# A small vision tower on one core: layer 0's attention outputs and sums computed by token, divided there and turned

## The reference

```python
def _L0_attn_ref(hidden_states, Wq, Wk, Wv, Wo):      # 16 heads of 16
    q = proj(Wq) * d ** (-0.5)
    k = proj(Wk)
    v = proj(Wv)
    s = jnp.einsum('bhqd,bhkd->bhqk', q, k)
    attn = 1.0 + s + 0.5 * s * s
    attn = jnp.where(causal, attn, 0.0)
    o = jnp.einsum('bhqk,bhkd->bhqd', attn, v)
    z = jnp.sum(attn, axis=-1, keepdims=True) + EPS   # 1e-6
    o = o / z
    y = o.transpose(0, 2, 1, 3).reshape(b, t, dim)
    return y @ Wo.T
```

## Time and profile before

| | us |
|---|---|
| median of 3 runs | 287.32 (284.48 to 288.15) |
| the profiled execution | 285.78 |
| its span | 284.1 |
| mean granted clock of PE, share of full | 0.988 |

### The profile page before, as it was taken

One profiled execution on the slowest core, in us unless ns is written; L12 is line 12 of the kernel. 1 busy time (PEld: TensorE's weight loads), 2 busy tenths in 40 slices (PEclk: granted clock), 3 DMA queues, 4 the chain that ended last, 5 costly groups with the idle time before them and its releaser, 6 DMA issues.

```text
span 284.1 us, 8057 instructions
## 1 busy us (share of the span) xinstructions
PE 250.1 (88%) x3292; PEld 197.7 (70%) x3292; DVE 182.9 (64%) x347; ACT 152.0 (54%) x322; POOL 157.2 (55%) x227
## 2 busy tenths in 40 slices
PE   0779989957999899897997899999999997988983
PEld 0667878845888688686886788888888884434331
DVE  0534628511559999999998588988777785534111
ACT  1312102056898868776765166675657653833450
POOL 7441324544374988787889556868676661145000
PEclk9999999999999999999999689999999999999999
DMA  5899430000000000000000000000000000002021
GB/s 176 202 248 310 106 98 0 3 0 0 3 2 2 0 2 2 2 2 3 3 2 0 2 2 2 3 3 2 3 2 5 2 3 2 0 0 68 0 66 44
DMA packets 9897, 9.81 MB, mean 35 GB/s; under 512 B 4303, under 2 KB 9030, under 8 KB 9862
## 3 DMA queue, kind: packets, MB, share of 16 engines
q1 hardware_dynamic: 9446, 9.31, 12.1%
q10 hardware_dynamic: 416, 0.01, 0.1%
HBM read 8.07 MB, written 1.25 MB: 33 GB/s over the span
## 4 chain that ended last, share of the span: by engine, by line
PE 58%; DVE 26%; issue 6%; ACT 5%; DMA 2%; POOL 2%; ACTq 0%; DVEq 0%; POOLq 0%
PE psum L1262 11%; PE psum L1298 7%; PE psum L1462 5%; PE psum L1445 5%; DVE img L1025 4%; DVE big L1018 4%; PE psum L1545 4%; PE psum L1520 3%; PE psum L1608 3%; PE psum L1596 3%; PE psum L1234 3%; DVE st L979 2%; PE psum L1535 2%; DMA w_raw<-in_L_tok_W 2%; DVE xq L1066 2%
## 5 line engine op out<-in xcount | busy, mean ns | idle before, releaser
L1298 PE MATMUL psum<-hnT,a 128*128 128x114 f32 x352 | 49.2, 284 | 1.6 <-ACT mT L695 1.2
L1298 PEld LDWEIGHTS psum<-hnT,a 128*128 128x128 f32 x352 | 44.0, 195 | 5.8 <-issue 2.1
L464 POOL TENSOR_SCALAR ve<-mvs 114x1 f32<-114x1 f32 x44 | 18.6, 422 | 52.1 <-DVE mvs L981 50.7
L1262 PE MATMUL psum<-wT,patchT 128*114 128x256 f32 x132 | 33.0, 405 | 1.6 <-DVE patchT L935 0.8
L459 POOL TENSOR_SCALAR big<-mT,parmask 128x228 f32<-128x228 f32 x22 | 22.8, 1047 | 20.9 <-ACT mT L665 20.9
L465 POOL TENSOR_TENSOR rstd<-ve,nhalf 114x1 f32<-114x1 f32 x44 | 27.8, 631 | 3.7
L485 POOL TENSOR_TENSOR big<-big,img 114x912 f32<-114x912 f32 x11 | 22.4, 2039 | 12.3 <-ACT big L729 12.3
L1262 PEld LDWEIGHTS psum<-wT,patchT 128*114 128x114 f32 x132 | 24.4, 191 | 7.0 <-DVE patchT L935 2.1
L1018 DVE SCALAR_TENSOR_TENSOR big<-big,img 114x912 f32<-114x912 f32 x11 | 17.5, 1590 | 14.8 <-ACT big L719 14.8
L719 ACT ACTIVATE big<-psum 114x912 f32<-114x912 f32 x22 | 19.3, 928 | 6.1 <-PE psum L1344 5.9
L979 DVE BATCH_NORM_STATS2 st<-h_all 114x6 f32<-114x256 f32 x44 | 18.8, 428 | 1.5
(11 more groups left out here) (156 smaller groups left out, 557.6 us busy)
## 6 DMA issues: line engine op xcount, KB each, us to landing
img<-in_x SPq DMA_DIRECT2D x6, 576.0 KB, 10.1
out<-h_all SPq DMA_DIRECT2D x10, 114.0 KB
w_raw<-in_L_tok_W SPq DMA_DIRECT2D x1, 768.0 KB, 5.9
a_raw<-in_L_attn_Wq SPq DMA_DIRECT2D x1, 256.0 KB, 8.5
a_raw<-in_L_attn_Wk SPq DMA_DIRECT2D x1, 256.0 KB, 8.6
a_raw<-in_L_attn_Wv SPq DMA_DIRECT2D x1, 256.0 KB, 8.7
a_raw<-in_L_attn_Wo SPq DMA_DIRECT2D x1, 256.0 KB, 11.9
qw<-in_L_ffn_weight SPq DMA_DIRECT2D x1, 256.0 KB, 12.0
```

The lines of the kernel that those rows point to most:

```text
L464: step(nc.gpsimd.tensor_scalar(ve[:, t:t + 1], mvs[:, t, 1:2], LN_EPS, None, ALU.add))
L1262: last = nc.tensor.matmul(EB[t % 2][0:T, 0:D], patchT[:, c, FIRST[t]:FIRST[t] + TI, :].rearrange("p b s -> p (b s)"), wT[:, c, :], start=( ...
L1298: return nc.tensor.matmul(bk[:, m * T:(m + 1) * T], w[:, c, m * 128:(m + 1) * 128], hnT[:, c, :], start=(c == 0), stop=(c == DC - 1))
```

## The change

In layer 0 the operands of the value product change places. The weights of a head (`E3[t % 3][:, n, :]`, 114x114) are now stationary, and the head's values move: `vO`, 17 columns a head, of which the last is one. So a single matmul a head gives, with tokens on partitions, 16 output columns and the sum in the 17th (`NB0`, 114 x 16 x 17 in PSUM). `sums0` and `take_z` are gone. DVE's `divide` adds 2e-6 to the 16 sums of a token, takes their reciprocal and multiplies them into the outputs, to `o_tok` in SBUF. PE turns `o_tok` by two transposes (`turn_o`, behind `v_proj0` or `v_proj`), and ACT copies the result into `oT` (`take_oT0`, behind `take_v0` or `take_v`). The wait for POOL's half of the mask stands before the ninth head. Two zeroings on POOL before the loop are gone (2304 columns each), one of 544 columns is new, and `q_proj0`'s copies and the mask lie elsewhere in the same buffer. The diff's core:

```diff
-        vX = sb("vX", [T, H * (128 + HD)])
+        vO_ = sb("vO", [T, 2, H * (HD + 1)])
+        vO = [vO_[:, n, :].rearrange("p (h q) -> p h q", q=HD + 1) for n in range(2)]
+        z0 = sb("z0", [T, H])
+        o_tok = sb("o_tok", [T, D])
...
-        OB0, ZB0 = bank[6][:, 0:DC * T], bank[6][:, DC * T:2 * DC * T]
+        NB0 = bank[6][0:T, 0:H * (HD + 1)].rearrange("p (h q) -> p h q", q=HD + 1)
+        OB0 = bank[6][:, H * (HD + 1):H * (HD + 1) + DC * T]
...
-            nc.gpsimd.memset(vX[:, :], 0.0).then_inc(consts, 1)
+            nc.gpsimd.memset(vO_[:, :, :], 1.0).then_inc(consts, 1)
...
-            def take_z(t):
-
-                act.wait_ge(z_ps, t + 1)
-                ge(act, lay[0]["oT"], t)
-                nc.scalar.activation(zT[:, :, :], ZB0.rearrange("p (c t) -> p c t", c=DC), ACT.Identity,
-                                     bias=eps0[:, :]).then_inc(z_sb, 1)
+            def take_oT0(t):
+                L = lay[0]
+                act.wait_ge(o_turn, t + 1)
+                ge(act, L["y_ps"], t)
+                nc.scalar.activation(oT[:, :, :], OB0.rearrange("p (c t) -> p c t", c=DC), ACT.Copy
+                                     ).then_inc(L["oT"], 1)
...
             def divide(t):
                 L = lay[0]
-                dve.wait_ge(z_sb, t + 1)
-                step(nc.vector.reciprocal(zT[:, :, :], zT[:, :, :]))
-                ge(dve, L["y_ps"], t)
-                nc.vector.tensor_tensor(oT[:, :, :], OB0.rearrange("p (c t) -> p c t", c=DC), zT[:, :, :], ALU.mult
-                                        ).then_inc(L["oT"], 1)
+                dve.wait_ge(L["oT_ps"], t + 1)
+                step(nc.vector.tensor_scalar(z0[:, :], NB0[:, :, HD], 2e-6, None, ALU.add))
+                step(nc.vector.reciprocal(z0[:, :], z0[:, :]))
+                ge(dve, o_turn, t)
+                nc.vector.tensor_tensor(o_tok[:, :].rearrange("p (h d) -> p h d", h=H), NB0[:, :, 0:HD],
+                                        z0[:, :].rearrange("p (h o) -> p h o", o=1).to_broadcast([T, H, HD]),
+                                        ALU.mult).then_inc(o_norm, 1)
...
             def values0(t):
                 L = lay[0]
                 pe.wait_ge(e_dve, t + 1)
-                pe.wait_ge(e_pool, t + 1)
                 pe.wait_ge(L["v_sb"], t + 1)
+                ge(pe, o_norm, t)
                 ge(pe, L["oT"], t)
+                for n in range(H):
+                    if n == H // 2:
+                        pe.wait_ge(e_pool, t + 1)
+                    r, c, odd = n // 4, n // 2 % 2, n % 2
+                    h = c * HC + 2 * r + odd
+                    last = nc.tensor.matmul(NB0[:, h, :], E3[t % 3][:, n, :], vO[t % 2][:, h, :], start=True, stop=True)
+                last.then_inc(L["oT_ps"], 1)
+
+            def turn_o(t):
+                pe.wait_ge(o_norm, t + 1)
+                ge(pe, lay[0]["oT"], t)
                 for c in range(DC):
-                    for odd in range(2):
-                        for r in range(4):
...
+                    last = nc.tensor.transpose(OB0[:, c * T:(c + 1) * T], o_tok[:, c * 128:(c + 1) * 128],
+                                               ident[0:T, 0:T])
+                last.then_inc(o_turn, 1)
...
                     values0(t)
-                    sums0(t)
...
                         v_proj0(t + 2)
+                        turn_o(t)
                         q_proj0(t + 2)
                     else:
                         v_proj(i)
+                        turn_o(t)
                         s_proj(i)
```

More of the change, by code:

```diff
@@ L115, in vit_tower @@
         img_ = img[:, 0, :, :].rearrange("p c n -> p (c n)")
[L116 to L124, removed]
+        qX = img_[:, 0:2 * DC * T].rearrange("p (c o t) -> p c o t", c=DC, o=2)
+        at = 2 * DC * T
+        maskT = img_[0:T, at:at + T]
         E3 = [big[0:T, n, :].rearrange("p (h t) -> p h t", h=H) for n in range(3)]
@@ L214, in vit_tower @@
         LN2 = math.log(2.0)
-        CONSTS = 9
+        CONSTS = 8
         POOL_STEPS = 17
@@ L262, in vit_tower @@
         e_pool = sem("e_pool")
-        z_ps = sem("z_ps")
-        z_sb = sem("z_sb")
+        o_norm = sem("o_norm")
+        o_turn = sem("o_turn")
         names = ["hn", "hnT_ps", "hnT", "m_ps", "m_sb", "mX", "s_ps", "s_sb", "v_ps", "v_sb", "sc",
@@ L421, in _ @@
             pool.wait_ge(by_patch_act, 1)
-            nc.gpsimd.memset(vX2[1][:, :], 0.0).then_inc(consts, 1)
-            nc.gpsimd.memset(eps0[:, :], 2e-6)
-            nc.gpsimd.memset(oneX[:, :], 0.0)
             step(nc.gpsimd.memset(maskT[:, :], 1.0))
-            nc.gpsimd.memset(oneX[:, HD:2 * HD], 1.0)
             for i in range(1, TI):
@@ L456, in expand @@
                 ge(pool, L["sc"], t)
-                pool.wait_ge(z_ps, NT - 1)
+                pool.wait_ge(lay[0]["oT_ps"], NT - 1)
                 for o in range(2):
@@ L710, in take_v0 @@
                 ge(act, L["oT_ps"], t - 1)
-                nc.scalar.activation(vX2[t % 2][:, :].rearrange("p (h q) -> p h q", h=H)[:, :, 0:HD],
+                nc.scalar.activation(vO[t % 2][:, :, 0:HD],
                                      VB0[0:T, :].rearrange("p (h d) -> p h d", h=H), ACT.Copy).then_inc(L["v_sb"], 1)
@@ L716, in square @@
                 act.wait_ge(L["sc"], t + 1)
-                ge(act, z_ps, t - 2)
+                ge(act, L["oT_ps"], t - 2)
                 for n in range(2):
@@ L771, in layer0 @@
                         square(t + 1)
-                    take_z(t)
                     if t >= 4 and t % 2 == 0 and t < NT - 1:
@@ L782, in layer0 @@
                         take_v0(t + 2)
+                        take_oT0(t)
                     else:
@@ L1351, in values0 @@
                 pe.wait_ge(e_dve, t + 1)
-                pe.wait_ge(e_pool, t + 1)
                 pe.wait_ge(L["v_sb"], t + 1)
+                ge(pe, o_norm, t)
                 ge(pe, L["oT"], t)
-                for c in range(DC):
-                    for odd in range(2):
-                        for r in range(4):
[L1358 to L1372, removed]
+                for n in range(H):
[8 more added lines that the diff above has]
+                ge(pe, lay[0]["oT"], t)
+                for c in range(DC):
+                    last = nc.tensor.transpose(OB0[:, c * T:(c + 1) * T], o_tok[:, c * 128:(c + 1) * 128],
+                                               ident[0:T, 0:T])
+                last.then_inc(o_turn, 1)
             def out_proj0(t, done=0):
@@ L1406, in product @@
                     pe.wait_ge(lay[0]["oT"], NT)
-                    pe.wait_ge(z_sb, NT)
                 else:
```

## The result

| | median us | ratio to before, 95% interval | span of the profiled run | mean granted clock |
|---|---|---|---|---|
| before | 285.9 | | 284.1 | 0.988 |
| after | 320.5 | 1.123 (1.114 to 1.133) | 318.3 | 0.911 |

The change costs 34.6 us, in the direction that was forecast and nearly three times the 12.7 of the forecast.

What follows compares the result with a forecast made beforehand. PE was taken to bound t = 0 to 3, DVE t = 4 to 9. Terms +6.9, +4.4 and +1.4 made +12.7 us, giving 298.5 from the profiled 285.8 or 300.0 from the median; forecast 299, range 293 to 306.

Steps and rivals of the forecast that it cites:

- Which way, and where: Whole kernel: slower by 12.7 us, +6.9 in t = 0 to 3, +4.4 in t = 4 to 9, +1.4 in t = 10.
- The pace of a load: Value matmuls on PE: each record is paced by its weight load, 0.100 us, so 32 take 3.20 us.
- x: PE work added per layer-0 iteration: 3.20 for the new values, less 1.72 removed, plus 0.25 for turn_o, 1.73 us.
- The reserve: PE's idle time in t = 4 to 9 that added work can use up: 50.8 elapsed against 44.8, 6.0 us.
- DVE, ACT, the round trip: Layer-0 loop: divide falls from 1.97 to about 0.94 us, ACT's exchanged copy costs nothing, waits on o_norm are covered.
- t = 10: The loop's last iteration: ACT's copy of the turned quantised inputs comes later, +1.4 us.
- The drop behind t = 10: Half-clock stretch of 6.8 us after the waits around 156 us, costing 3.2 us, assumed to recur; without it 296 us.
- the clock falls inside the values: Rival: streaming 17 columns per load drops the clock, half of the loop at half clock, +24, 322 us; chance 0.07.
- the rival of loads at 0.065 to 0.08: Rival: value loads at that pace, partly hidden, so costs meet the reserve, -6 to 293 us; chance 0.06.
- 11x - 6.3: Short form of the whole kernel's change in us, with x the PE work added per iteration; +12.7 at x = 1.73.

Runs made afterwards that it cites:

- half_load: The changed kernel, each value matmul loading the weights of only 57 of the 114 tokens, other tokens' outputs and sums left out; 282.5 us, 0.986 of before.
- v64_heads: The changed kernel with three small things moved and 64 moving columns a value matmul instead of 17; 295.5 us, 1.036 of before.
- before_short_recip: The kernel before, with divide's reciprocal taken over 16 of the 228 columns, so most sums are not inverted; 282.8 us, 0.986 of before.
- split4: The changed kernel with its sixteen value matmuls in four pieces of four heads between dense work, turn_o and its copy later; median 323.3 us.
- quad_v17: The changed kernel with three small things moved and each head's weights loaded in four column groups, 17 moving columns; 293.1 us, 1.022 of before.

## Why the prediction was wrong, point by point

- **Which way, and where.** Right. PE became the bound of t = 0 to 9, DVE's relief only paid for part of it, nothing behind the loop absorbed it.
- **The pace of a load.** Right: 0.101 us a record in after against 0.100. half_load confirms that it goes by the load's columns. The Trainium skill's estimate of 95 ns (TensorE: Matmul & The Clock Gate, "LDWEIGHTS") was 6% low.
- **x.** Right within 0.1: 8.27 - 6.61 = 1.66 at full clock against 1.73. In v64_heads the values took 3.24, not 3.20, the turn 0.20 (77.31 to 77.51), not 0.25, and the rest of the iteration closed up by 0.06.
- **The reserve.** Right as used. t = 4 to 9 of v64_heads take 55.3, the sum had 55.2. It is not DVE's alone, though: DVE's relief without more PE work gets back 3.0 of its 6.0 (before_short_recip).
- **DVE, ACT, the round trip.** Right. divide takes 0.92; PE waited 0.2 us for `oT` once in the loop and never for `o_norm`.
- **t = 10.** +0.7 at full clock against 1.4. By an estimate from its clock of 0.96, before lost 0.5 us of clock in this stretch, which the sum did not take out.
- **The drop behind t = 10.** I let it recur. The rest was 2.3 us shorter than before in after and 2.6 in v64_heads, so of its 3.2 us most did not.
- **The clock.** This is the step that failed. I gave "the clock falls inside the values" 0.07, and wrote against it that the drop of before came after real idling. So the sum priced 32 records of 17 columns by their loads alone and put nothing for what they do to the clock. From one drop behind idle time I took idle time for its only cause. In after PE was busy in 39.66 of 39.66 us, and the clock was at 0.83. The rival's own price, half of the loop at half clock, +24 and 322 us, came out at 50 us at half, +23.8 and 320.5. The rival's mechanism and its size were both right; that the two times agree within 2 us is in part luck, since the half of the loop was a guess. The range ended at 306, short of it.
- **Two slips in the sums.** The range is said to hold the missing clock drop, but without the drop x at its low end gives 291, below 293. And the rival of loads at 0.065 to 0.08 comes by 11x - 6.3 to +0.4 to +5.7, that is 286 to 293 us; its "-6 to 293" is no result of that sum. Neither bears on the outcome.

By the profile's busy time PE had no gap in t = 0 to 3 of after (39.66 of 39.66 us), and the clock was at 0.83; v64_heads, as busy (33.06 of 33.06), kept it at 1.00. The Trainium skill's table at the end of TensorE: Matmul & The Clock Gate ("Why this matters for your kernels") advises keeping TensorE busy and free of longer idle gaps to avoid such drops. The traces show that this was not enough here.

The values and sums took 1.72 us in the form of before and 3.22 in that of the change. That bears out the rule of the Trainium skill that I quoted against the orientation (TensorEngine Tiling (Array Packing), "When to Use Tiling"): with few moving columns, swap the operands and tile the narrow one by columns. It does not hold against every form, though. With the wide operand loaded in column groups the same heads took 1.97 and, in four groups where PE did not stand still, 1.19, less than the 1.72.

## What to carry to other kernels

A matmul with a wide stationary operand and few moving columns costs its weight load, here 0.101 us a record for 114 fp32 columns, two records a matmul; load it in column groups, side by side. Before such a rewrite read not only whether PE is busy but what it streams. If the granted clock falls though PE is busy, useless moving columns under the same loads are one way to win it back: here 64 in place of 17 added 0.02 us to the 3.22 of sixteen heads and took the kernel from 318 to 295 us. Loading in column groups was another, and a better one (284 to 286). Spreading the sparse matmuls among dense ones was not enough (309 and 323).

## What the runs showed of the hardware that I had not expected

- The granted clock fell to half again and again while PE was busy: 0.83 with PE busy in 39.66 of 39.66 us, about 50 us at half clock in the loop's 124.6.
- Once down it could stay down for long, 20 us in split4 (0.50 over 19.5 us), and the same kernel ran through once at 1.0.
- Loads into different column groups overlap: 64 records of 64 and 50 columns in 1.97 us, 128 of 32 and fewer in 1.19.
- PE can stand still for 0.5 to 2.5 us amid a run of short records with no releaser shown, 8.1 us in quad_v17's loop.
